# When GpSimd issues its gathers in a fill: new release points, and the single-column gathers moved

## The reference

```
V = emb_v[x]                        # 32 x 2048 x 64
VV = V[i] * V[j]                    # 496 pairs
hid = relu(VV @ at_w + at_b)
score = hid @ at_h
pooled = sum over pairs of VV * score
out = sigmoid(pooled @ p + w0 + sum over fields of w1[x])
```

## Time and profile before

| | before |
|---|---|
| median of three executions | 862.96 us |
| the profiled execution's own time | 866.6 us |
| its span in the trace | 864.8 us |
| TensorE matmuls busy | 804.1 us (93%) |
| VectorE busy | 700.3 us (81%) |
| ScalarE busy | 642.8 us (74%) |
| GpSimd busy | 608.3 us (70%) |

### The profile page before, as it was taken

How to read it: one execution, slowest core, us unless ns; L and a number is a source line. 1 busy time by engine, 2 the same in 40 slices (tenths; PEclk the granted TensorE clock), 3 DMA queues, 4 the chain that set the end, 5 groups by cost and what they waited for, 6 DMA issues and landing times.

```text
span 864.8 us, 30490 instructions
## 1 busy us (share of the span) xinstructions
PE 804.1 (93%) x12600; PEld 348.1 (40%) x12600; DVE 700.3 (81%) x1175; ACT 642.8 (74%) x672; POOL 608.3 (70%) x574
## 2 busy tenths in 40 slices
PE   0775969999999999999999999999999999999998
PEld 0232424444434444443444444444444444344443
DVE  3647757889888888889888889898888898888883
ACT  0552747878878778878777878887778788777875
POOL 6771477777778776777787778777787777677740
PEclk9898989999999999999999999999999999999999
DMA  5897437884523543223414421458714532224100
GB/s 33 59 75 98 141 27 25 24 23 22 22 19 19 24 24 22 21 22 20 21 16 24 24 22 16 23 24 21 24 16 24 24 23 21 21 21 22 10 1 2
DMA packets 34722, 24.21 MB, mean 28 GB/s; under 512 B 24776, under 2 KB 24845, under 8 KB 34701
## 3 DMA queue, kind: packets, MB, share of 16 engines
q0 software_dynamic: 17920, 17.08, 40.5%
q1 hardware_dynamic: 16133, 6.82, 3.0%
q10 hardware_dynamic: 648, 0.03, 0.0%
HBM read 20.59 MB, written 3.31 MB: 28 GB/s over the span
## 4 chain that ended last, share of the span: by engine, by line
PE 85%; SPq 5%; DMA 4%; POOL 4%; issue 2%; ACT 0%; DVE 0%; POOLq 0%
PE Z L529 49%; PE SG L544 26%; PE SG L559 5%; SPq L228 5%; POOL rows L262 4%; PE Z L493 4%; DMA joined<-in_L_rec_emb_v_dram 1%; DMA table<-joined 1%; DMA rows<-in_L_rec_emb_v_dram,idx 1%; DMA rows<-table,joint_idx 0%; DMA idx_raw<-in_r_x_dram 0%; PE Z L614 0%; SPq L214 0%; PE Z L602 0%; SPq L225 0%
## 5 line engine op out<-in xcount | busy, mean ns | idle before, releaser
L395 DVE TENSOR_TENSOR X<-V 128x992 f32<-128x992 f32 (+15 forms) x1024 | 636.9, 693 | 56.9 <-PE Z L529 31.0
L262 POOL DMA_INDIRECT rows<-table,joint_idx x464 | 510.7, 1101 | 193.1 <-issue 122.8
L470 ACT ACTIVATE H<-Z,bias 128x1024 f32<-128x1024 f32 x512 | 536.1, 1118 | 142.3 <-PE Z L529 138.9
L529 PE MATMUL Z<-X,w_sb 64*64 64x512 f32 x4096 | 476.1, 601 | 11.4 <-issue 8.3
L529 PEld LDWEIGHTS Z<-X,w_sb 64*64 64x64 f32 x4096 | 155.1, 133 | 244.2 <-issue 238.6
L544 PE MATMUL SG<-H,score_w 128*32 128x496 f32 (+15 forms) x4096 | 249.3, 383 | 1.0 <-issue 1.0
L544 PEld LDWEIGHTS SG<-H,score_w 128*32 128x32 f32 x4096 | 109.8, 110 | 206.4 <-issue 111.8
L421 ACT ACTIVATE pV<-V,pmask 128x1024 f32<-128x1024 f32 x64 | 80.8, 1266 | 0.1
L364 DVE TENSOR_TENSOR prod<-SG,gram 128x496 f32<-128x496 f32 x32 | 21.6, 675 | 69.8 <-PE SG L544 69.8
L410 ACT COPY V<-Z 128x1024 f32<-128x1024 f32 x31 | 31.4, 1013 | 51.6 <-PE Z L493 51.6
L559 PE MATMUL SG<-V,pV 128*32 128x32 f32 x4096 | 58.3, 200 | 11.5 <-issue 7.5
(11 more groups left out here) (39 smaller groups left out, 21.6 us busy)
## 6 DMA issues: line engine op xcount, KB each, us to landing
rows<-table,joint_idx POOLq DMA_INDIRECT x464
table<-joined SPq DMA_DIRECT2D x2, 1584.0 KB
joined<-in_L_rec_emb_v_dram SPq DMA_DIRECT2D x12, 256.0 KB, 16.7
rows<-in_L_rec_emb_v_dram,idx POOLq DMA_INDIRECT x48, 4.9
w_all<-in_L_rec_w_dram,idx POOLq DMA_INDIRECT x48
idx_raw<-in_r_x_dram SPq DMA_DIRECT2D x4, 64.0 KB, 2.2
table<-tail SPq DMA_DIRECT2D x1, 54.7 KB
tail<-in_L_rec_emb_v_dram SPq DMA_DIRECT2D x1, 53.0 KB
```

The lines of the kernel that those rows point to most:

```text
L262: pool.indirect_dma_start(out=rows[t % 2][:, g * FILL_M + m, half, c0:c1], out_offset=None, in_=source, in_offset=bass.IndirectOffsetOnAxi ...
L395: last_one = nc.vector.tensor_tensor(xo, vj, vi.unsqueeze(3).to_broadcast(shape), ALU.mult)
L470: nc.scalar.activation(H[:, s % H_SLOTS, :, COLS * g:COLS * g + COLS], Z[:, z_slot(r), :, :], ACT.Relu, bias=bias[:, 0:1]).then_inc(hid_re ...
L529: done = nc.tensor.matmul(Z[64 * par:64 * par + 64, z_slot(r), half, :], w_sb[k, :], X[k, s % X_SLOTS, par, COLS * g:COLS * g + COLS], sta ...
```

## The change

The release of the first group no longer waits for round 15 of fill t-3 but for its score step 4, the first of the two that stand between round 15 and the grams. The other groups are released after 3, 7 and 10 rounds of fill t-2, where they were released after 4, 8 and 12. The plain `w1` gather behind each fill's gathers is gone: 16 of the 48 now stand between the gathers of fill 2 and the wait for the table, and the other 32 behind the gathers of the last fill.

```diff
-PACE, PACED_FROM, PACED_EVERY = 2, 16, 4
+GROUP_AFTER = (0, 3, 7, 10)
...
                 for g in range(2):
                     for m in range(FILL_M):
-                        if paced and m % PACE == 0:
-                            pool.wait_ge(z_ready, ROUNDS * (t - 3) + PACED_FROM + PACED_EVERY * (FILL_M * g + m) // PACE)
+                        if paced and g == 0 and m == 0:
+                            pool.wait_ge(scored, STEPS * (t - 3) + LAST_STEPS[0] - 1)
+                        elif paced and m % 2 == 0:
+                            pool.wait_ge(z_ready, ROUNDS * (t - 2) + GROUP_AFTER[2 * g + m // 2])
...
             pool.wait_ge(first_turned, 2)
             gather(2)
+            gather_w1(GATHERS)
             pool.wait_ge(rows_turned, 1)
             pool.wait_ge(idx_ready, 4)
             pool.wait_ge(table_stored, 16 * 3)
...
                 gather(t, paced=True)
-                gather_w1(1)
             gather_w1(PLAIN_FILLS * GATHERS)
```

## The result

The changed kernel takes **849.64 us** (median of four, 848.76 to 851.74) beside 863.13 us before (median of four, 862.49 to 866.16); the ratio is 0.9832, 95% interval 0.9804 to 0.9859, 12 to 17 us less. The forecast of 861.0 had the sign and a seventh of the size, and the range of 853 to 868 didn't hold it.

What follows compares the result with a forecast made beforehand. TensorE was taken to bound the kernel, losing 16.1 us to stalls when gathers start in the grams. Terms of -2.4 us (grams) and +0.5 us (start-up) gave -1.9 us, so 861.0 us on the median 862.96; range 853 to 868.

Steps and rivals of the forecast that it cites:

- What bounds the kernel: TensorE's order of work or the start-up; gathers starting in the grams stall its issue, 16.1 us lost over 28 fills.
- the release latency: First group: an idle released GpSimd starts 0.30 us after, putting the first gather 0.4 us ahead of the grams.
- The sum: Stalls in the grams: 21 sets at 0.65 us make 13.7 us against 16.1 now, so -2.4 us.
- The 0.65 us a set: Stall cost of grams with no gather held: 0.05 + 0.27 + 0.27 + 0.06 us, bounds 0.55 and 0.85.
- The held sets: Grams during which a gather is held by VectorE's products and nothing stalls: about 7 of 28.
- near tie: A gather starting close to a small product's start is held 4 times in 29; two such places a fill expected.
- rival B: Most grams free as gathers lose to VectorE's products: half held 856.5 us, all held 847.4; chance 0.17.
- Other groups: Later groups' gathers, released earlier in the fill, cost nothing in TensorE's rounds and scores, and none becomes late.
- Start-up: 16 w1 gathers beside the table's loads delay fill 3's rows: +0.5 us, bounds 0 and +5.
- rival D: The table is late in the start-up: +5 us, 865.5 us and up; chance 0.06.
- Rival C: First gather waits about 0.27 us for the next large product, giving three whole stalls in the grams: 867.8 us; chance 0.20.
- Rival E: Placing gathers is worth nothing, as the stalls come from TensorE's own issue: 863.5 us; chance 0.10.

Runs made afterwards that it cites:

- Waits first: Changed kernel with GpSimd's two waits for the rows buffer in their own instruction ahead of the wait for score step 4: 870.86 us, ratio 1.0020.
- first pair: The first measurement of the unaltered changed kernel beside the kernel before: 849.64 us against 863.13, ratio 0.9832.
- w1 alone: Kernel before with only the w1 gathers moved, all release points as before: 859.66 us, ratio 0.9954.
- release alone: Kernel before with only the release points changed, one w1 gather a fill kept: 847.80 us, ratio 0.9817; on another chip 853.26 us, ratio 0.9808.
- behind the grams: Changed kernel with the first group released by round 0 of the next fill, the others by rounds 4, 8 and 11: 850.06 us, ratio 0.9847.

## Why the prediction was wrong

- **What bounds the kernel** held: the stalls are in the 28 sets of grams, and rounds and scores show no new ones. Fills without a stall now take 24.50 us (232.82 - 208.32) and 24.1, as priced.
- **The step that failed is the release latency**, "a released GpSimd that is idle starts 0.30 us after". It is 0.81 us for the first gather of a fill. The 0.30 came from group releases with one wait. In the trace of before the first gather of a fill never stood idle at the head of the queue, as the w1 gather went ahead, so its price wasn't in any row I used and should have been bounded. From -0.4 us it went to +0.13. "Waits first", where it is 0.30, takes 870.86 us beside 858.90: this one number hid 12 us. For the profiled executions the stalls in the 28 sets come to 15.2 us there and 2.1 in the changed kernel of the first pair.
- **The sum with that number right.** "Waits first" takes 841.42 - 145.52 = 695.9 us for the 28 fills, 1.2 less than before, where the sum said 2.4 less. That the total comes so near is in part luck, see the held sets below.
- **The 0.65 us a set** held for the place it was made for: the sets of "waits first" mostly take 1.71 to 1.75 us from first to last matmul, 0.60 to 0.64 over 1.11. The first stall of the set was absorbed, as taken.
- **The held sets**, 7 of 28 taken as free, were mis-sized. In "waits first" the first gather, at -0.38 us, always gets in at the next start of a product, 0.04 to 0.28 us off, and no gather of the fills is held to a row's end. Four sets have no stall above 0.05 us, each because GpSimd's second gather came 0.26 us or more late behind one of its idle times in "issue". The near tie itself was a weak reading: in the trace of before the four held gathers start 0.024 to 0.041 us behind a product's start, and the 13 that went through 0.028 to 0.037, so the distance doesn't part them. What came in most fills, a gather that waits, is rival B's event, but not by its reason. At +0.13 us a large product has just begun, and the gather waits for the next or for the end of the row, 1.08 to 1.16 us off. At a place read 0.5 us off I saw no such wait.
- **Other groups:** no cost, as said. The w1 gathers out of the fills: counted at nothing but the place, and "w1 alone" bears it out with 4 us. The idle times of GpSimd that come with them weren't foreseen.
- **Start-up:** +0.5 taken, bounds 0 and +5. By the start of fill 3 the runs gave from -3.4 (first pair) to +2.9 and +6.0. Where it is a loss, the table's loads are delayed, as in rival D; in the medians it hides behind the gain in the fills.
- **Rival C** had the wait for the next product right at the predicted place (0.18 us in the set shown), but not the first stall made whole by it: in "waits first" one set of 28 shows anything of it, 0.1 us. **Rival E** is refuted: 0.5 us in the place of one gather a fill is worth 12 us. Whether the Trainium skill's sentence that TensorE never waits on anyone in SBUF (SBUF — State Buffer, "SBUF: two separate sides") holds here, no run shows: the stalls stand in the rows as "issue", and what inside TensorE's issue a gather stops stays open.

## What to carry to other kernels

Where one engine issues a burst of tiny instructions, look at what starts on the others in that microsecond, and place it by a semaphore. Work out the release latency from a gather with the same number of waits, not from any gather. And move one thing at a time: here the release points alone are worth 0.018 to 0.019, the w1 gathers alone 0.005, and beside the new release points the moved w1 gathers add nothing and cost 5.6 us on one chip.

## What the runs showed that I had not expected

- A gather whose release passes through a separate wait instruction starts 0.80 to 0.82 us after the releasing matmul (changed kernel, release alone, behind the grams); one that holds its only wait itself, 0.29 to 0.31 us (the kernel before and "waits first").
- Each gather that works in the grams stops TensorE's issue twice: once ending 0.11 to 0.21 us after its start, once 0.28 to 0.36 us ahead of its end. The second moves with the gather's wait for VectorE; that is what takes it out of the grams.
- A gather that waits is let in at the next start of a product (24 of 24 and 25 of 25 in the two traces of release alone) or only at the end of VectorE's row (20 of 24 in the changed kernel), at the same place. What decides between the two isn't shown.
- With 16 gathers a fill GpSimd stands in "issue" for 0.6 to 5.3 us at four to eight places of a run, with 17 at none.
- On two chips a train of gathers slowed 128 matmuls to 8.2 us, with stalls of 1.16 us, and the kernel before took 1350 us.
